# An attention kernel over 16 images: the loop over images 1 to 14 written out as straight code on all engines

## What is computed

```python
wp = normalize_weight(w_proj)[:, :, 0, 0] / fan_in
wo = normalize_weight(w_out)[:, :, 0, 0] / fan_in
xf = x.reshape(B, C, N)
h = jnp.einsum('oc,bcn->bno', wp, xf)
qkv = h.reshape(B, N, n_heads, 3 * d_k)
q, k, v = jnp.split(qkv, 3, axis=-1)
q = pixnorm(q) * scale
k = pixnorm(k) * scale
v = pixnorm(v)
attn = jnp.einsum('bihd,bjhd->bijh', q, k)
attn = jax.nn.softmax(attn, axis=2)
res = jnp.einsum('bijh,bjhd->bihd', attn, v)
res = res.reshape(B, N, C)
res = jnp.einsum('oc,bnc->bon', wo, res).reshape(B, C, H, W)
return (a_c * x + b_c * res) / div
```

## Time and profile before

| | us |
|---|---|
| median of 3 runs | 3130.0 |
| lowest and highest | 3126.65, 3157.09 |
| profiled execution | 3130.55 |
| its span, first to last instruction | 3128.4 |
| PE busy | 2989.1 (96%) |
| DVE busy | 2596.4 (83%) |
| ACT busy | 2403.5 (77%) |
| POOL busy | 480.7 (15%) |
| mean granted clock of TensorE | 0.983 of full |

### The profile page before, as it was taken

The page is one execution under the profiler, slowest core; times in us unless marked ns, Lnnn a source line. Parts: engine busy times, 40 slices in busy tenths (PEclk is TensorE's granted clock), DMA queues, the critical chain, the costliest instruction groups (busy, mean ns, idle before and its releaser), DMA issues.

```text
span 3128.4 us, 90952 instructions
## 1 busy us (share of the span) xinstructions
PE 2989.1 (96%) x36928; PEld 2037.3 (65%) x36928; DVE 2596.4 (83%) x3197; ACT 2403.5 (77%) x2993; POOL 480.7 (15%) x678
## 2 busy tenths in 40 slices
PE   6999999999999999999999999999999999999997
PEld 5676666666666666666666666666676666766664
DVE  5898878978788887888878888788887878878986
ACT  5887877878777777777778778687786877868785
POOL 0211121112111121112111121111211121111210
PEclk9999999999999999999999999999999999999999
DMA  3224324242243322334233342332423224243133
GB/s 99 50 40 81 72 36 106 43 87 61 41 101 55 80 59 50 89 60 85 49 61 77 60 85 49 69 76 53 92 53 77 66 46 102 46 76 72 39 76 92
DMA packets 459647, 212.32 MB, mean 68 GB/s; under 512 B 407952, under 2 KB 407952, under 8 KB 459152
## 3 DMA queue, kind: packets, MB, share of 16 engines
q1 hardware_dynamic: 459152, 205.58, 31.2%
HBM read 71.30 MB, written 33.55 MB: 34 GB/s over the span
## 4 chain that ended last, share of the span: by engine, by line
PE 86%; issue 4%; DMA 3%; DVE 3%; ACT 2%; POOL 1%; SPq 0%; ACTq 0%; DVEq 0%
PE ps_pv L932 24%; PE ps_score L911 21%; PE ps_dense L889 12%; PE ps_dense L893 11%; PE ps_dense L891 10%; PE ps_dense L948 3%; PE ps_dense L950 3%; PE ps_dense L949 3%; DMA out<-x_res 1%; DMA x_res<-in_x 1%; DVE probs L724 1%; ACT e_tile L530 1%; DVE x_res L751 0%; DVE probs L715 0%; ACT x_res L557 0%
## 5 line engine op out<-in xcount | busy, mean ns | idle before, releaser
L530 ACT ACTIVATE e_tile<-ps_score,shift 128x1024 f32<-128x1024 f32 x1024 | 1121.5, 1116 | 461.3 <-PE ps_score L911 337.3
L724 DVE TENSOR_TENSOR probs<-e_tile,probs 128x1024 f16<-128x1024 f32 x1024 | 1248.1, 1231 | 69.6 <-ACT probs L537 59.5
L932 PEld LDWEIGHTS ps_pv<-v_pair,probs 128*128 128x128 f16 x24576 | 785.4, 98 | 157.8 <-issue 134.5
L911 PE MATMUL ps_score<-qkT 64*128 64x512 f16 x6144 | 771.8, 385 | 101.4 <-issue 84.1
L932 PE MATMUL ps_pv<-v_pair,probs 128*128 128x65 f16 (+1 forms) x24576 | 832.6, 194 | 3.6 <-DVE probs L724 2.6
L889 PE MATMUL ps_dense<-wpT_hi,x_hi 128*128 128x512 f32 x1536 | 640.9, 417 | 8.5 <-ACT arena L498 3.5
L893 PE MATMUL ps_dense<-wpT_hi,x_lo 128*128 128x512 f32 x1536 | 603.1, 393 | 0.0
L891 PE MATMUL ps_dense<-wpT_lo,x_hi 128*128 128x512 f32 x1536 | 601.2, 391 | 0.0
L911 PEld LDWEIGHTS ps_score<-qkT 64*128 64x128 f16 x6144 | 262.7, 95 | 459.4 <-issue 191.6
L537 ACT ACTIVATE probs<-e_tile 128x1024 f16<-128x1024 f32 x512 | 541.6, 1058 | 24.4 <-ACT e_tile L530 0.4
L715 DVE CAST probs<-e_tile 128x1024 f16<-128x1024 f32 x512 | 356.8, 697 | 172.3 <-PE ps_pv L932 109.9
(11 more groups left out here) (50 smaller groups left out, 1750.0 us busy)
## 6 DMA issues: line engine op xcount, KB each, us to landing
x_raw<-in_x SPq DMA_DIRECT2D x128, 256.0 KB, 3.2
x_res<-in_x SPq DMA_DIRECT2D x128, 256.0 KB, 3.2
out<-x_res SPq DMA_DIRECT2D x128, 256.0 KB, 2.7
arena<-in_w_proj SPq DMA_DIRECT2D x24, 128.0 KB, 3.1
qkT<-arena SPq DMA_TRANSPOSE x128, 5.5
resT<-res_split SPq DMA_TRANSPOSE x128, 3.4
arena<-in_w_out SPq DMA_DIRECT2D x1, 1024.0 KB, 8.1
```

The source lines that it names most:

```text
L530: act.activation(e_tile[:, t % 2, :, :], ps_score[:, t % 2, :, :], ACT.Exp, bias=shift[:, 0:1], scale=1.0 / (QK_UP * QK_UP)).then_inc(exp_ ...
L724: dve.tensor_tensor(probs_of(b, t, 1), e_tile[:, t % 2, :, :], probs_of(b, t, 0), ALU.subtract).then_inc(probs_low, 1)
L911: mm = pe.matmul(ps_score[:, t % 2, h, :], k[rows, k_part, :], q[rows, :, q_part, :], start=(i == 0), stop=(i == 2))
L932: mm = pe.matmul(ps_pv[:, h, o:o + n], probs_of(b, t, part)[:, h, queries], v[:, cols], start=(j == 0 and it == 0 and part == 0 and cols.s ...
```

## The change

The loop of the four engines is replaced by what SP had already: `body(b)` is called for b = 1 to 14 when the program is built, so its code stands there 14 times, and b is a number.

```diff
             body(0, prev=False)
-            if eng is nc.sync:
-                for b in range(1, B - 1):
-                    body(b)
-            else:
-                with eng.Fori(1, B - 1) as b:
-                    body(b)
+            for b in range(1, B - 1):
+                body(b)
             body(B - 1, nxt=False)
```

## The result

The changed kernel has a median of 3018.55 us (3018.03 to 3019.01, 4 runs), the one before in the same session 3128.45 us. The ratio is 0.963, with a 95% interval from 0.957 to 0.968; that is wide because one of the four runs of before took 3157. The forecast was 3022 us, in a range from 3012 to 3046.

What follows compares the result with a forecast made beforehand. PE was taken as the bound, idled by its loop's jumps. Gaps of 84.1 us plus lower clock of 24.6 give 108.7 us off 3130.55, so 3021.9, taken as 3022 us, with an 80% range of 3012 to 3046.

Steps and rivals of the forecast that it cites:

- Gaps, 84.1 us: PE's 13 waits at the loop's jumps, ahead of score, 6.47 us each, would go: 84.1 us saved.
- the two borders without one: Loop entry at 242.87 and fall-through at 2932.42 have no gap on PE, so only the jump costs.
- Lower clock, 24.6 us: Thirteen stretches at PE's lower clock behind the gaps would go: 24.6 us saved.
- whole images: Lower-clock price from image lengths: images 2 to 13, less their gap, take 1.92 us more than image 1.
- the two groups: Alternative lower-clock price from twelve score matmuls and the next attend slot: 2.43 us per border, 31.6 in all.
- Register arithmetic, nothing: Removing the loop's register instructions on PE, ACT and DVE would gain nothing, at most 2.7 us.
- the 52 us of PE's queue: Time of PE's register instructions over 14 images, 116 per image at 32 ns, expected not to lie on the path.
- Instruction traffic: PE's loop code is already fetched anew per image, so straight code fetches no more: 18 or 19 blocks per image.
- starve PE: Rival: straight code waits at block borders on PE, up to 3.2 us each, about 3830 us; chance 3%.
- Image 1 as the measure: Each of the 14 images would take image 1's 184.35 us, 2580.9 in all.
- DVE's and ACT's pauses: DVE and ACT lose over 6 us of pause per image; claimed not needed, as their backlog stays the same without it.
- another engine or a transfer: Rival: another bound appears, nearest DVE's store, load, add on `x_res`; 67 us given back, 3089 us; chance 4%.

Runs made afterwards that it cites:

- e1: Against the kernel before, images 1 to 14 written out on PE alone, the other engines keeping their loops: 3021.2 us, ratio 0.966.
- e2: Against the kernel before, DVE, ACT and POOL written out, only PE keeping its loop: 3124.85 us, ratio 0.9986.
- e6: Against the changed kernel, PE looped with two images per turn (6 jumps), the other engines written out: 3064.94 us.
- e5_hint_slot100: The kernel before, loops kept, plus a prefetch hint on PE's branch and PE's loop head at slot 100 of a block: 3021.7 us, ratio 0.966.
- e7_pause: The changed kernel, with PE held up by eleven small GpSimd operations at the start of images 2 to 14: 3134.01 us.
- e12_all_written: The changed kernel itself, measured again on one chip with two partly looped kernels: 3019.44 us, ratio to before 0.9651.
- e9_slot200: The kernel before, with PE's loop head at slot 200 of a block of 256 instructions, no hint: 3093.25 us.
- e4_slot0: The kernel before, with PE's loop head at the first slot of a block of 256 instructions, no hint: 3077.81 us.

## Why the prediction was right, point by point

- *Gaps, 84.1 us.* They went in full. That the jump was their cause I had argued from the two borders without one; e1, e2 and e6 show it, and e5_hint_slot100 shows that it is not the jump as such but the fetch of its target. One reading on the way was too generous. The 4% of "issue" in the chain (4.4% or 138 us unrounded) had the 84.1 us for its larger part only: after the change 1.8%, some 54 us, are still there, spread over pieces that I gave no owner.
- *Lower clock, 24.6 us.* In the two profiled executions the 14 images went from 2689.55 to 2581.19 us, which is 108.4; less 84.1 that leaves 24.3. The price that I took from whole images, 1.92 each, was nearer than the 2.43 from the two groups. e7_pause gives 2.2 per pause with no jump in it, where I had only the one kind of idle time to read.
- *Register arithmetic, nothing.* On PE that is right: with it (e5) 3021.7 us, without it (e1) 3021.2, and both have the other engines' loops. From image 1's first score matmul to image 15's it is 2582.69 us in e5_hint_slot100 and 2582.63 in e12_all_written. Of the 52 us of PE's queue nothing shows. One premise was wrong: I had written that the waits which stood as instructions of their own are now carried by the operation behind them. Some are, as the one for `qk_turned0`, but others had ridden on the register instructions, and PE has 337 separate wait instructions after the change where it had 169. They cost nothing that these traces show.
- *Instruction traffic.* As forecast, the blocks become fewer: 18 for image 2 of the changed kernel, where the earlier trace rows had 21 for image 1. Straight code doesn't starve PE here: none of its waits in the 14 images is put down to "issue", and its busy share of 99.8% leaves no place for one.
- *Image 1 as the measure.* 14 x 184.35 = 2580.9 was forecast, and 2581.19 came. The single images take from 183.99 to 185.11 us and don't grow from one to the next. DVE's and ACT's pauses were not needed. DVE is 87% busy in the 14 images (2249.35 of 2581.19), and PE's waits for `x_res` in L885 and L944 sum to 10.2 us in the whole kernel.
- *What was not in the sum.* The profiled execution came out at 3019.01 us, where 3021.9 was worked out. The head alone is 3.0 us shorter, 242.87 us before and 239.86 after. The edit doesn't touch that code. Its mean clock was 0.97 before and 0.99 after, and among the experiments, all with the same head, it took from 239.3 to 242.1 us. So this is scatter between executions. The tail was 0.5 us shorter, and the 14 images and what lies around the span together 0.65 us longer. The 3.5 us between the forecast of 3022 and the median of 3018.55 are of the size of the heads' scatter.
- *The rivals.* The mechanism of "another engine or a transfer" does exist, as a rare event: in e6_two_per_turn one load of `x_res` came 5.1 us late, and PE stood 2.7 us for it. It is not a rule of the faster pace, and in the changed kernel the longest such wait in the 14 images was 1.1 us.

## What to carry to other kernels

Where the bounding engine shows idle time that nothing explains, count it. As many gaps as a loop has jumps, and a long branch record, pointed here to an engine that waits for its own code. The time per jump was two things, the gap itself and a stretch at the lower clock, and a place where the loop is entered or left without a jump showed what an iteration costs without either. Writing the code out, or keeping the loop with a prefetch hint and its branch late in a block, came to the same time, and only the engine that is the bound needed it.

## What the runs showed that I had not expected

- The price of a jump depends on where the loop's head lies among the blocks of 256 instructions: 6.5 us of gap with a border right behind the head, 3.3 us with the head at slot 0. That is 51 us of the kernel's time (3129 to 3078) from placement alone, with not one instruction of the body changed.
- With the hint the branch took 1372 ns with the head left where it fell (the branch then stands about 118 instructions into its block, by my count), and 357 ns with the head at slot 100 (about 218). That fits a fetch that starts earlier against the branch, but the head's place changed with the branch's, and no run separates the two.
- It follows, though no run here tried it, that an edit ahead of the loop that adds or removes a few instructions on PE could move the kernel by up to these 1.6%.
- Pauses of 3.1 to 3.5 us lower the clock in some places only, 4 or 5 of 13 in two profiled executions, but 12 of 13 in e9_slot200 with gaps of 3.3 to 3.7 us. The time scatters with it: e4_slot0 took 3071.69 us in the run with a mean granted clock of 0.994 and 3083.09 in one with 0.989, while the changed kernel lay from 3018.03 to 3019.01 at 0.998 each time.
